# Second products of an image all given ahead of its successor's exponentials; projections between attention tiles; blocks around the transposes back

## The reference, cut to what matters

```python
def block(x):                                  # x: 8, 256, 32, 32
    n = layernorm_over_channels(x)
    qkv = conv1x1(n)                           # 768 channels
    agg = conv1x1_grouped(depthwise5x5(qkv))   # 768 channels
    for half in (qkv, agg):                    # heads of 8 channels
        q, k, v = relu(half.q), relu(half.k), [half.v, 1]
        kv = k^T v                             # per head
        o = q kv;  out = o[:-1] / (o[-1] + 1e-15)
    x = x + batchnorm(proj(out of both halves))
    t = layernorm_per_token(x)
    p = softmax(mean_tokens(t) @ router.T)     # one row per image
    w = weights of 6 experts from the top 2 of p
    return x + sum_e w[e] * (gelu(t @ W1[e] + b1[e]) @ W2[e] + b2[e])
```

## Time and profile before

| | |
|---|---|
| median of 3 runs | 1650.11 us (1649.84 to 1651.37) |
| the profiled execution | 1651.42 us, span in the profile 1649.7 us |
| PE busy | 1360.8 us, 82% |
| DVE busy | 1278.6 us, 78% |
| ACT busy | 1063.1 us, 64% |
| POOL busy | 972.8 us, 59% |
| mean granted clock of PE | 0.934 of 2.4 GHz |

### The profile page before, as it was taken

One profiled execution on the slowest core, in us unless ns is written; L12 is line 12 of the kernel. 1 busy time (PEld: TensorE's weight loads), 2 busy tenths in 40 slices (PEclk: granted clock), 3 DMA queues, 4 the chain that ended last, 5 costly groups with the idle time before them and its releaser, 6 DMA issues.

```text
span 1649.7 us, 18712 instructions
## 1 busy us (share of the span) xinstructions
PE 1360.8 (82%) x6844; PEld 786.7 (48%) x6844; DVE 1278.6 (78%) x1305; ACT 1063.1 (64%) x1855; POOL 972.8 (59%) x746
## 2 busy tenths in 40 slices
PE   4516647799888988799888988899888997999598
PEld 2315525455455545455455545555464445545343
DVE  4895999997969966996969966996969987970000
ACT  3434534677567775767567776777567866675476
POOL 3683626576487566576477566676476647444544
PEclk8756879899999999999999999899999999999899
DMA  5100000000001000010001100010001000100000
GB/s 180 77 2 25 26 0 1 1 27 13 1 1 39 31 9 1 0 64 14 1 1 39 39 1 1 1 39 13 1 1 39 13 1 1 39 13 1 0 14 26
DMA packets 14251, 32.75 MB, mean 20 GB/s; under 512 B 2384, under 2 KB 5328, under 8 KB 13904
## 3 DMA queue, kind: packets, MB, share of 16 engines
q1 hardware_dynamic: 14160, 31.56, 5.5%
HBM read 23.17 MB, written 8.39 MB: 19 GB/s over the span
## 4 chain that ended last, share of the span: by engine, by line
PE 46%; DVE 19%; ACT 19%; POOL 9%; issue 6%; DMA 1%; SPq 0%; POOLq 0%; ACTq 0%; DVEq 0%
PE wbk L533 19%; DVE dacc L1112 15%; PE acc L546 11%; PE wbk L625 6%; ACT gh L730 4%; ACT hb L731 4%; POOL dwo L930 3%; PE wbk L635 3%; ACT tapb L705 2%; POOL nrm L889 1%; PE wbk L584 1%; ACT hb L825 1%; PE wbk L611 1%; ACT dwo L700 1%; PE wbk L599 1%
## 5 line engine op out<-in xcount | busy, mean ns | idle before, releaser
L1112 DVE SCALAR_TENSOR_TENSOR dacc<-qkvs,dww,dacc 128x930 f32<-128x930 f32 (+4 forms) x954 | 1053.2, 1186 | 0.0
L960 POOL TENSOR_TENSOR gl<-hb,gh 128x512 f16<-128x512 f32 x256 | 304.4, 1191 | 419.1 <-ACT hb L731 418.2
L825 ACT ACTIVATE hb<-wbk,b1s 128x512 f32<-128x512 f32 x256 | 175.2, 684 | 156.3 <-PE wbk L533 156.2
L930 POOL TENSOR_TENSOR dwo<-dwo,tapb 128x992 f32<-128x992 f32 (+1 forms) x104 | 240.4, 2311 | 12.9 <-ACT tapb L705 9.7
L546 PE MATMUL acc<-gh,w2h 128*128 128x512 f16 x512 | 197.6, 386 | 33.5 <-ACT sum_b L764 30.6
L546 PE MATMUL acc<-gh,w2l 128*128 128x512 f16 x512 | 197.9, 387 | 0.0
L546 PE MATMUL acc<-gl,w2h 128*128 128x512 f16 x512 | 197.9, 386 | 0.0
L730 ACT ACTIVATE gh<-hb,ewg 128x512 f16<-128x512 f32 x256 | 182.3, 712 | 9.5 <-DVE ewg L1065 9.5
L533 PE MATMUL wbk<-th,w1h 128*128 128x512 f16 x512 | 154.2, 383 | 33.7 <-ACT qr L807 16.7
L731 ACT ACTIVATE hb<-hb,ewg 128x512 f32<-128x512 f32 x256 | 181.8, 710 | 0.0
L1016 DVE RECIPROCAL den<-den 128x128 f32<-128x128 f32 x32 | 30.4, 949 | 189.1 <-ACT den L804 189.1
(11 more groups left out here) (146 smaller groups left out, 2232.1 us busy)
## 6 DMA issues: line engine op xcount, KB each, us to landing
xa<-x SPq DMA_DIRECT2D x8, 1024.0 KB, 5.0
yr<-x SPq DMA_DIRECT2D x8, 1024.0 KB, 5.0
out<-yr SPq DMA_DIRECT2D x16, 512.0 KB, 2.8
dwo<-w SPq DMA_DIRECT2D x1, 2048.0 KB, 11.0
yr<-w SPq DMA_DIRECT2D x2, 1024.0 KB, 16.3
dwo<-w_qkv SPq DMA_DIRECT2D x1, 768.0 KB, 4.7
wp<-w_proj SPq DMA_DIRECT2D x1, 512.0 KB, 12.4
pw<-w_pw SPq DMA_DIRECT2D x16, 24.0 KB
```

Source lines behind the costliest of these rows:

```text
L825: last = nc.scalar.activation(hb[:, f % GB, :], b[:], ACT.Gelu, bias=b1s[:, f % FT:f % FT + 1], scale=1.0 / (X_SCALE * W_SCALE))
L930: ins = nc.gpsimd.tensor_tensor(d3[:, oy, ox], d3[:, oy, ox], t3[:, iy, ix], ALU.add)
L960: nc.gpsimd.tensor_tensor(gl[:, f % GB, :], hb[:, f % GB, :], gh[:, f % GB, :], ALU.subtract).then_inc(g_low, 1)
L1112: ins = nc.vector.scalar_tensor_tensor(out=dst[:, oy, ox], in0=i3[:, jy, jx], scalar=dww[:, m, tap:tap + 1], in1=a3[:, oy, ox], op0=ALU.mu ...
```

## The change

Three things are moved in the list; no instruction is added or taken away. First, `ffn` blocks: one block goes from between the tiles of `att(j-1,1)` to behind them, ahead of `back`; and one block of the new image goes ahead of `back(j,0)` and `logits`, where none was. Second, `qkv(j,0)` and `qkv(j,1)` go between the tiles of `att(j-1,1)`, and `qkv(j+1,2)` and `qkv(j+1,3)` between those of `att(j,0)`. Third, all seconds that are left of image j-2, and its `final`, are given ahead of `exp(j-1)`; the lag of the seconds is counted by `finished` from then on, so that they don't start on the next image earlier than before. Besides, `scale(j,0,0)` goes ahead of `rbc` and `apply`.

```diff
+    finished = [0]
-    def second(k):
-        s, n = stream[k]
+    def second():
+        s, n = stream[finished[0]]
+        finished[0] += 1
...
-                if i >= LAG:
-                    second(i - LAG)
+                if i - finished[0] >= LAG:
+                    second()
...
             fill(1)
+            qs = qkv(j, 0) + qkv(j, 1) if d else []
             for t in range(TT):
                 give(("att", new, 1, t))
-                if t in (2, 5):
+                if t == 2 or (t == 5 and not d):
                     fill(1)
+                if t in (1, 4, 5, 7):
+                    give(*qs[:1])
+                    del qs[:1]
...
-            fill(1)
+            fill(2)
             give(("back", new, 1, 0, 0), ("back", new, 1, 0, 1))
...
-            give(*[("att", j, 0, t) for t in range(4)], n=n)
-        if c:
-            fill(1 if d else 2)
+        ks = qkv(nxt, 2) + qkv(nxt, 3) if c and a else []
+        for t in range(TT if d else 0):
+            give(("att", j, 0, t), n=n)
+            if t in (1, 2, 5, 7):
+                give(*ks[:1])
+                del ks[:1]
+            if t == 3:
+                give(("scale", j, 0, 0))
+                if c:
+                    give(("rbc", new, 1, 0), ("rbc", new, 1, 1), ("apply", new, 1, 0), ("apply", new, 1, 1))
...
             give(("low", new, 1, 0), ("low", new, 1, 1))
-            if a:
-                give(*qkv(nxt, 2))
+            fill(1)
...
             give(("logits", new))
-            if a:
-                give(*qkv(nxt, 3))
-            else:
-                fill(1)
             fill(left(new - 1) + 2)
+            while finished[0] < new * (NCH * FT):
+                second()
             give(("exp", new))
```

More of the change, by code:

```diff
@@ L163, in schedule @@
             give(("scale", new, 1, 1))
+            if d:
+                add_base(j, 0)
         if j == 0:
@@ L166, in schedule @@
                 give(*group)
-        if d:
+        if j == 0:
             give(*qkv(j, 0), *qkv(j, 1), n=n)
             add_base(j, 0)
-            if j == 0:
-                for group in norm_in(1)[2:]:
-                    give(*group, n=n)
+            for group in norm_in(1)[2:]:
+                give(*group, n=n)
         out = norm_out(nxt) if a else [[], [], []]
@@ L200, in schedule @@
             fill(1)
-        if d:
-            give(*[("att", j, 0, t) for t in range(4)], n=n)
-        if c:
-            fill(1 if d else 2)
+        ks = qkv(nxt, 2) + qkv(nxt, 3) if c and a else []
[8 more added lines that the diff above has]
+                    give(("rbc", new, 1, 0), ("rbc", new, 1, 1), ("apply", new, 1, 0), ("apply", new, 1, 1))
+        if c and not d:
+            fill(2)
             give(("rbc", new, 1, 0), ("rbc", new, 1, 1), ("apply", new, 1, 0), ("apply", new, 1, 1))
-        if d:
-            give(("scale", j, 0, 0))
-            give(*[("att", j, 0, t) for t in range(4, TT)], n=n)
         if c:
@@ L266, in schedule @@
     give(("gsplit",) + stream[-1])
-    for i in range(k - LAG, k):
-        second(i)
+    while finished[0] < k:
+        second()
     return o
```

## The result

The changed kernel took 1709.47 us (median of 4 runs, 1707.58 to 1710.06), the kernel before 1650.74 us on the same chip (4 runs, 1649.84 to 1654.32). The ratio is 1.035, with a 95% interval of 1.0332 to 1.0368. The profiled execution took 1710.06 us.

A forecast was written before the change was run, and what follows sets the result against it. PE bounds the kernel, by its own work in order plus gaps where ACT or POOL are late. Rounds 2 to 5 (36.8) and others 7.2 + 5 + 5 + 6.5 make 60.5; 1650.1 + 60.5 = 1711 us, range 1678 to 1738.

The forecast's parts named there:

- projections among `att(2,1)`: On PE among these attention tiles: waits for projection copies make the phase lose 2.3 instead of 1.12 us, taken as +1.05.
- first `ffn(2,0)`, its wait: PE arrives at 13.3 us, ahead of `back(3,0)`, and waits 7.5 us for POOL's low parts, ready at 20.85.
- half clock behind it: Behind PE's 7.5 us wait for the low parts, two products run at clock 0.50, adding 2.6 us.
- third `agg` tile: PE waits 2.4 us for the first tile's bank, which ACT copies only after `final`, a table load and the exponentials.
- gelu, `gl`: PE waits 1.25 us at `ffn(2,4)` for a gelu, then 1.35 us at the first second product for `gsplit` and POOL's part.
- half clock in the string: Short successive PE gaps from the `agg` tiles to `stats` lower the clock: +2.0 us, between 0 and 4.
- round 1, 6, 7, 8: Rounds outside 2 to 5, costed separately: about 5, 7.2, about 5 and 6.5 us more than before.
- gaps traded, clock spared: Rival: wait at `ffn(2,0)` but no clock fall in the later short gaps; some 4 us a round, 1675 to 1690; chance 0.18.
- The clock stays down: Rival: PE at half clock from the 7.5 us wait to `ffn(2,5)`, some 12 more a round, about 1785; chance 0.07.
- The gap is simply filled: Rival: 5.85 us wait goes, nothing replaces it, if low parts are ready by about 14; about 1580, or 1645; chance 0.06.
- This is the term that decides: Said of the block ahead of `back(3,0)`: PE waits 7.5 us for low parts, delaying transposes, logits and router.
- the old gap: PE's 5.85 us wait for `final` at image 2's first second product, before the change; with half clock, 8.5 us a round.

The follow-up runs named there:

- `final` early: Kernel before, with the old image's last two second products and `final` one block earlier, behind `ffn(s,2)`: 1647.06 us, ratio 0.9975.
- weights early: Kernel before, with only DVE's maximum at tap 73 instead of 76 and route at tap 80 instead of 84: 1649.76 us, ratio 0.9993.
- the last step: Kernel before with `final` one block earlier, `squares` and `sums` ahead of `ffn(s,2)`, plus DVE's maximum and route three and four taps earlier: 1627.86 us, ratio 0.987.
- with the projection besides: Kernel before with last two second products and `final` one block earlier, and `qkv(nxt,3)` also ahead of `back`: 1645.38 us, ratio 0.9961.
- with `squares` early: Kernel before with last two second products and `final` one block earlier, and both `squares` and `sums` of image j+2 ahead of `ffn(s,2)`: 1642.46 us, ratio 0.9932.

## Why the prediction was right

The forecast was 1711 us and 60.5 us more than before; it came to 1709.5, 58.7 more. Point by point, in its own steps (round 3 unless another is named):

| step | predicted | measured |
|---|---|---|
| projections among `att(2,1)` | +1.05 | +1.03 |
| denominators of tile 3 copied | 6.2 | 5.88 |
| PE done with tiles and projections | 13.3 | 13.07 |
| first `ffn(2,0)`, its wait | 20.85, 7.5 | 20.66, 7.59 |
| half clock behind it | +2.6 | +1.85 (+2.5 in rounds 2 and 4) |
| third `agg` tile | 2.4 | 1.95 |
| gelu, `gl` | 1.25, 1.35 | 0.43 (1.04 in rounds 2 and 4), 0.98 |
| first second product | 46.9 | 46.49 |
| `rb`, other half of `stats` | 2.35, 0.45 | 2.23, 1.18 (none in rounds 2 and 4) |
| half clock in the string | +2.0 | +1.7 |
| `ffn(2,5)` | 54.6 + 2.0 of clock = 56.6 | 55.27 |
| weights ready | 43.5 | 41.4 |
| rounds 2 to 5 | 4 x 9.2 = 36.8 | 33.3 |
| round 1, 6, 7, 8 | 5, 7.2, 5, 6.5 | 6.4, 9.9, 4.7, 4.6 |

The mechanism held at every place of rounds 2 to 5. No one term was far off; nearly all were a little long, so that the sixth block came at 55.2 to 55.3 and not at 56.6. Half rate for the whole block behind the 7.5 us wait is what rounds 2 and 4 show (2.5 us); in rounds 3 and 5 the last half of its second product was at full rate (1.85). For the string I took 2.0 of clock, and it is some 1.7 in each of them: in `stats`, where I had it, in rounds 2 and 4 (3.65 and 3.64 us), and ahead of it in rounds 3 and 5, there with the `agg` tiles at 3.09 instead of 2.05 and the first product behind them at 1.06 and 0.83 instead of 0.59 for two matmuls. The third `agg` tile, the gelu and `gl` wait 0.2 to 0.45 us less than I had. Against that, 0.4 to 0.6 us more is lost later in the round, at a wait for `sv` that I did not have.

Two hits are in part luck. The parts that I name for the projections among `att(2,1)` add up to +1.17 and not to the +1.05 that I took; and measured, the three waits are 0.20 us each and not 0.34, while the first gap at `back(2,1)`, which I said would stay, grew from 1.33 to 1.58. And the sum is nearer than its terms: rounds 2 to 5 were forecast 3.5 us too high and round 8 1.9, rounds 1 and 6 together 4.1 too low.

Round 6 went the other way. I had the gap of every full round in mind, but before it was 3.71 there and not 5.85, so the change had less to give back; and new waits of 0.65 and 1.66 us stand at `gl` and a gelu, and that for the copy of `vt` is 1.59 instead of 1.33. In round 8 DVE waits 10.8 us longer for the logits (about 10 was forecast), and 4.6 of it remained, not 6.5.

Of the rivals, **gaps traded, clock spared** fell: its place for the saved time was the string, and each of rounds 2 to 5 has half clock in it. **The clock stays down** fell too: the clock is 1.00 from 697 to 707, and the 0.50 behind the wait of 1.95 us stands from 709 to 711, with 0.70 and 0.59 in the microsecond ahead of it and behind it. The Trainium skill's page "TensorE: Matmul & The Clock Gate", section "HAM oscillation — how this bites in real kernels", describes waits between bursts that throttle PE each time; the trace agrees that each long wait does so, but the clock is back before the next wait comes, so 1.85 to 2.5 us are paid at this gap and not the whole stretch. I had read into that section that the low clock lasts from one wait to the next; it describes only that each wait starts a new throttled stretch. **The gap is simply filled** had its condition right: the low parts came at 20.5, not by 14. And the table switch cost 1.29 us from load to exponential, as in the earlier trace rows; the drain that "ScalarE: Activation LUTs", section "What ACT_TABLE_LOAD costs", adds for every switch in the Trainium skill has no row here, and with it the time would by my estimate have been some 20 us longer than it was.

One sentence of the prediction needs a limit. "This is the term that decides" is true of the cost of the block where it stands alone (44 us of 59), and not of what its removal gives: 17.5 us. The three parts do not add. From the kernel before, projections cost 2.9 us a round, the loop ahead of `exp` then 3 more, the block 2.5 more: 184.6, 187.5, 190.5, 192.9. The block alone costs 6. My reading of this, argued from the waits and not isolated by a run, is that each part makes PE late by filling or moving PE's own work against the same two chains, DVE to POOL to the low parts, and DVE's router to ACT to `gl`. Where one part already waits for a chain, the next is paid only in what it adds to it.

Of the old gap I said in the rivals that with the weights from DVE still binding only 1645 would be reached. The last runs bear that out: `final` early gave 1647, weights early 1650, both with `squares` moved as well 1628. The expectation that both come within a few tenths was wrong, since the weights alone took 1.8 us off the gap. But neither that rival nor an expectation had the other half of the last step: where POOL worked while DVE made the weights, DVE needed up to 4.1 us more for them. What remains open is how much of the last step is the gap and how much the clock, since no run holds the clock fixed; and whether `squares` are needed for it, since weights and `final` without them were not tried.

## What to carry to other kernels

Before a block of work is put into a place to fill a gap, ask when its own inputs are ready there: the first product of an image was ready at 20.7 us and was put at 13.1, and all that stood behind it on the in-order queue paid. Price the parts of an edit together and not one by one: of three parts that cost 59 us together, taking away the one that costs 44 alone gave back 17. And move all the chains that end at a gap: one alone gave nothing or 0.25%, `final`, sums and router together 1.3%. When work is moved to an engine that is idle, look at what the other engines do in that stretch: with the sums and `final`'s addition on POOL in its stretch, DVE's router took 4.1 us longer.

## What the runs showed of the hardware that was not expected

- DVE's short instructions can take much longer while POOL works. The fifteen of the router took 3.40 to 3.43 us in every round of every run in which POOL was idle or nearly so. With POOL busy for 1.3, 2.5 and 4.8 us of their time they took 4.2, 5.2 to 5.5 and 7.6 us (the runs with `final` early, with the projection besides, and with `squares` early). All that POOL did in these stretches were the additions of `sums` and `final`, both of two 32-bit operands; no other kind of POOL work was tried there, and what in them holds DVE up is not shown.
- Short gaps lower the clock as well. Behind waits of 1.95, 1.05, 0.99 and 2.22 us, with work between them, the granted clock was 0.50 for the next 2 us and `stats` took 3.44 instead of about 2; behind 2.08 and 2.25 us, 4.2 us apart, a first product ran at half rate too.
- It is not the same in each execution, nor in each round. One program had a granted clock of 0.943 in 1652.91 us and 0.935 in 1667.2 us, and another had rounds of 183.4 and 185 us in turn, by whether the transposes behind a gap of 2.11 us ran at half rate. So an edit that takes 1.8 us off a gap can measure as nothing.
- A longer gap did not cost more clock. Behind 7.59 us half rate added 1.85 or 2.5 us by the round; behind 5.85 us, in the kernel before, 1.2 and 1.4; behind 4.02 us, in round 3 of the run with the router alone, PE went on at 0.38 us a matmul for two of them and then fell to 0.63, and 1.6 us were added.
- The clock can fall while PE waits (0.81 over the gap of 7.59 us) or only once it works again (1.00 up to the end of the gap of 4.02 us, then 0.66 and 0.50 in the next stretches of 2 us).
